# The last layer of a graph transformer: row normalisation, routing and ranking rearranged over the engines

## The reference

```python
def _layernorm(x, axis=-1, eps=1e-05):
    m = jnp.mean(x, axis=axis, keepdims=True)
    v = jnp.var(x, axis=axis, keepdims=True)
    return (x - m) / jnp.sqrt(v + eps)

probs = jax.nn.softmax(xf @ switch_w + switch_b, axis=-1)     # xf: 1250 normalised rows
prob_max = jnp.max(probs, axis=-1)
routes = jnp.argmax(probs, axis=-1)
sort_idx = jnp.lexsort((-prob_max, routes))
...
rank = jnp.zeros((N,), jnp.int32).at[sort_idx].set(rank_sorted.astype(jnp.int32))
keep = rank < capacity                                        # capacity 195 of 1250 rows
...
h = jax.nn.gelu(jnp.einsum('ecd,edf->ecf', buf[:E], w1) + b1[:, None, :], approximate=False)
o = jnp.einsum('ecf,efd->ecd', h, w2) + b2[:, None, :]
y = jnp.where(keep[:, None], y_exp, xf)
out = y * prob_max[:, None]
```

## Time and profile before

| | us |
|---|---|
| median of 3 runs | 1721.52 (1719.59 to 1725.29) |
| the profiled execution, its own time | 1720.55 |
| its span in the profile | 1718.8 |
| mark of tile 0 to start of `ranked` (L1703) | 1454.43 to 1559.10 |
| behind it, up to the end of the span | 159.7 |

### The profile page before, as it was taken

How to read it: one execution, slowest core, us unless ns; L and a number is a source line. 1 busy time by engine, 2 the same in 40 slices (tenths; PEclk the granted TensorE clock), 3 DMA queues, 4 the chain that set the end, 5 groups by cost and what they waited for, 6 DMA issues and landing times.

```text
span 1718.8 us, 25251 instructions
## 1 busy us (share of the span) xinstructions
PE 1582.5 (92%) x9809; PEld 1196.0 (70%) x9809; DVE 1135.0 (66%) x2618; ACT 680.6 (40%) x1359; POOL 412.0 (24%) x251
## 2 busy tenths in 40 slices
PE   3979999999989889999999999998999999986987
PEld 2556666555655568887888888888888976666664
DVE  6777664114466989898988697668765833785223
ACT  4421001122232466667767664336534521441110
POOL 3788888888400000000000000000000000002331
PEclk9999999999999999999999999999999999996999
DMA  9335535454752422223420264336312224645951
GB/s 360 83 60 118 119 77 118 61 92 74 198 178 85 143 76 84 88 80 102 134 81 28 64 191 144 125 108 202 131 47 79 88 83 146 220 180 201 315 160 50
DMA packets 194889, 213.67 MB, mean 124 GB/s; under 512 B 81359, under 2 KB 149597, under 8 KB 194770
## 3 DMA queue, kind: packets, MB, share of 16 engines
q1 hardware_dynamic: 118146, 187.01, 33.0%
q0 software_dynamic: 75760, 22.70, 8.3%
q10 hardware_dynamic: 864, 2.36, 0.4%
HBM read 144.74 MB, written 68.40 MB: 124 GB/s over the span
## 4 chain that ended last, share of the span: by engine, by line
PE 53%; POOL 16%; DVE 13%; DMA 7%; issue 6%; ACT 4%; SPq 0%; POOLq 0%; ACTq 0%; DVEq 0%
PE bank L1073 20%; POOL table L2117 16%; PE bank L902 6%; PE bank L904 6%; PE bank L903 6%; DMA table<-amount,place 4%; PE bank L1243 4%; PE bank L1231 3%; PE bank L1127 3%; PE bank L1099 2%; DVE junk L1478 2%; PE bank L1142 1%; DVE eb L1513 1%; PE bank L1112 1%; DVE eb L1522 1%
## 5 line engine op out<-in xcount | busy, mean ns | idle before, releaser
L1073 PE MATMUL bank<-hb,eb 128*128 128x193 f32 (+3 forms) x2400 | 417.7, 331 | 12.7 <-ACT node L1920 7.6
L1073 PEld LDWEIGHTS bank<-hb,eb 128*128 128x128 f32 (+3 forms) x2400 | 400.3, 190 | 23.3 <-issue 10.3
L2117 POOL DMA_INDIRECT table<-amount,place x170 | 346.9, 2040 | 73.3 <-issue 49.1
L2123 POOL IOTA iota8i<- 128x8 int32 x1 | 0.1, 140 | 952.7 <-DMA node_rows<-node 952.7
L1513 DVE SCALAR_TENSOR_TENSOR eb<-shift_b,as_low,shift_b 128x640 f32<-128x640 f32 (+1 forms) x240 | 196.5, 861 | 0.3 <-PE bank L1073 0.2
L1906 ACT ACTIVATE eb<-eb,asd 128x640 f32<-128x640 f32 (+1 forms) x240 | 181.4, 812 | 28.7 <-DVE eb L1513 28.7
L1478 DVE CUSTOM_DVE_ANT_0 junk<-ab,absent 128x1250 bf16<-128x1250 f32 x120 | 174.2, 1452 | 1.1
L1522 DVE SCALAR_TENSOR_TENSOR eb<-eb,count 128x1280 f32<-128x1280 f32 (+1 forms) x120 | 174.6, 1455 | 0.0
L902 PE MATMUL bank<-wg_hi,x1T_hi 128*128 128x384 bf16 (+3 forms) x360 | 118.6, 329 | 0.3 <-DVE x1T_lo L1345 0.3
L903 PE MATMUL bank<-wg_lo,x1T_hi 128*128 128x384 bf16 (+3 forms) x360 | 118.6, 329 | 0.0
L904 PE MATMUL bank<-wg_hi,x1T_lo 128*128 128x384 bf16 (+3 forms) x360 | 118.6, 329 | 0.0
(11 more groups left out here) (290 smaller groups left out, 3011.2 us busy)
## 6 DMA issues: line engine op xcount, KB each, us to landing
w<-in_w SPq DMA_DIRECT2D x16, 1152.0 KB, 10.1
shift_b<-shift_rows SPq DMA_DIRECT2D x24, 625.0 KB, 5.7
h_rows<-h_row SPq DMA_DIRECT2D x27, 388.0 KB
hb<-h_rows SPq DMA_DIRECT2D x12, 873.0 KB
ar<-node_rows SPq DMA_DIRECT2D x27, 384.0 KB
table<-zero POOLq DMA_DIRECT2D x3, 3054.0 KB, 19.0
tab<-table SPq DMA_DIRECT2D x27, 312.5 KB, 3.7
qk_rows<-qk_row SPq DMA_DIRECT2D x12, 625.0 KB
```

The costliest lines, as they stand in the source:

```text
L1073: ins = T.matmul(bank[w // 2][0:M, c0:c0 + GC + 1], p[0:K, u, w * P:w * P + M], hv[0:K, t, 0:GC + 1], start=opens and u == 0 and w % 2 == ...
L2117: G.indirect_dma_start(tables[i], bass.IndirectOffsetOnAxis(place[:, c:c + 1], axis=0), amount16[:, c:c + 1], None, compute_op=ALU.add).th ...
```

## The change

Four things change, all in the last layer.

1. The reciprocal root. Before, six small VectorE operations on one column (L1633 to L1643) made it, and VectorE then made the normalised row (L1645). Now there are five small ones, three of which take other columns as per-partition scalars, and the last makes the bias -mean/root. ScalarE makes the normalised row, as Identity with scale and bias from those columns.
2. The bias of the switch is added by TensorE, as a seventh matmul of each tile's logits with a row of ones. VectorE's addition and the step `logits` on VectorE go; `route` reads the logits from `bank`.
3. `rank` makes one comparison over all rows so far (larger or equal) in place of two (larger or equal for earlier tiles, larger for its own), and subtracts from the own tile's count the ties that are not earlier, by a mask with values 0 and -1.
4. Waits and counts are renumbered to match.

```diff
                 for k in range(KD):
-                    ins = T.matmul(bank[2][0:R, 0:EXPERTS], fT[t % 2][:, k, 0:R], sw[:, k, :], start=k == 0,
-                                   stop=k == KD - 1)
-                ins.then_inc(sem["logit_mm"], 1)
+                    T.matmul(bank[2][0:R, 0:EXPERTS], fT[t % 2][:, k, 0:R], sw[:, k, :], start=k == 0, stop=False)
+                T.matmul(bank[2][0:R, 0:EXPERTS], ones[0:1, 0:R], sbias[0:1, :], start=False,
+                         stop=True).then_inc(sem["logit_mm"], 1)
...
-                V.tensor_scalar(v, v, LN_EPS, None, ALU.add).then_inc(sem["x2_norm"], 1)
+                V.tensor_scalar(v, v, LN_EPS, -1.0, ALU.add, ALU.mult).then_inc(sem["x2_norm"], 1)
                 ve.wait_ge("x2_root", t + 1)
                 V.reciprocal(r, u).then_inc(sem["x2_norm"], 1)
                 ve.wait_ge("x2_norm", n + 2)
-                V.tensor_tensor(u, v, r, ALU.mult).then_inc(sem["x2_norm"], 1)
+                V.tensor_scalar(u, v, r, r, ALU.mult, ALU.mult).then_inc(sem["x2_norm"], 1)
                 ve.wait_ge("x2_norm", n + 3)
-                V.tensor_tensor(u, u, r, ALU.mult).then_inc(sem["x2_norm"], 1)
+                V.tensor_scalar(r, u, 3.0 / ROOT, r, ALU.add, ALU.mult).then_inc(sem["x2_norm"], 1)
                 ve.wait_ge("x2_norm", n + 4)
-                V.tensor_scalar(u, u, -0.5, 1.5, ALU.mult, ALU.add).then_inc(sem["x2_norm"], 1)
-                ve.wait_ge("x2_norm", n + 5)
-                V.tensor_tensor(r, r, u, ALU.mult).then_inc(sem["x2_norm"], 1)
-                ve.wait_ge("x2_norm", n + 6)
-                V.tensor_scalar(xf[0:R, t, :], x2[0:R, t, :], stats3[0:R, t, 12:13], stats3[0:R, t, 14:15],
-                                ALU.subtract, ALU.mult).then_inc(sem["xf_ready"], 1)
+                V.tensor_scalar(v, mean, -1.0, r, ALU.mult, ALU.mult).then_inc(sem["x2_norm"], 1)
...
             def route(t):
...
+                V.tensor_reduce(most, out, AX.X, ALU.max).then_inc(sem["route_v"], 1)
                 ve.wait_ge("iota_f", 3)
-                V.tensor_tensor(lg[0:R, t, :], bank[2][0:R, 0:EXPERTS], sbias[0:R, :],
-                                ALU.add).then_inc(sem["route_v"], 1)
...
-                for p0, p1, op, j in ((0, lo, ALU.is_ge, 0), (lo, hi, ALU.is_gt, 1)):
-                    if p1 > p0:
-                        ins = V.scalar_tensor_tensor(won[0:R, p0:p1], pr[0:R, p0:p1], prob, mate[0:R, p0:p1], op,
-                                                     ALU.mult, accum_out=cnt[0:R, j, t:t + 1])
-                ins.then_inc(sem["ranks"], 1)
+                V.scalar_tensor_tensor(won[0:R, 0:hi], pr[0:R, 0:hi], prob, mate[0:R, 0:hi], ALU.is_ge, ALU.mult,
+                                       accum_out=cnt[0:R, 0, t:t + 1]).then_inc(sem["ranks"], 1)
...
             def new_norm(t):                                  # ScalarE
-                se.wait_ge("x2_norm", 6 * t + 1)
-                A.activation(stats3[:, t, 15:16], stats3[:, t, 13:14], ACT.Sqrt).then_inc(sem["x2_root"], 1)
+                R = rows(t)
+                se.wait_ge("x2_norm", NORM_STEPS * t + 1)
+                A.activation(stats3[:, t, 15:16], stats3[:, t, 13:14], ACT.Sqrt, scale=-ROOT).then_inc(sem["x2_root"], 1)
+                se.wait_ge("x2_norm", NORM_STEPS * (t + 1))
+                A.activation(xf[0:R, t, :], x2[0:R, t, :], ACT.Identity, bias=stats3[0:R, t, 13:14],
+                             scale=stats3[0:R, t, 14:15]).then_inc(sem["xf_ready"], 1)
```

More of the change, by code:

```diff
@@ L60 @@
 WEIGHT_SETS = 5
-ROUTE_STEPS, RANK_STEPS = 7, 4
+ROUTE_STEPS, NORM_STEPS, RANK_STEPS = 6, 5, 4
+ROOT = 2.0 ** (2 / 3)
 OUT_ROWS = 4
@@ L616, in program @@
         lg, ex = put("lg", [P, NT, EXPERTS]), put("ex", [P, NT, EXPERTS])
-        earlier = put("earlier", [P, P])
+        uncount = put("uncount", [P, P])
         stats3 = put("stats3", [P, NT, 16])
@@ L727, in program @@
         even, win = put("even", [P, P], BF16), put("win", [P, P], BF16)
-        cnt = put("cnt", [P, 3, NT])
+        cnt = put("cnt", [P, 2, NT])
         signs = put("signs", [P, 2], BF16)
@@ L1629, in new_norm @@
                 R = rows(t)
-                v, r, u = (stats3[:, t, i:i + 1] for i in (13, 14, 15))
-                n = 6 * t
+                mean, v, r, u = (stats3[:, t, i:i + 1] for i in (12, 13, 14, 15))
+                n = NORM_STEPS * t
                 ve.wait_ge("x2", 3 * (t + 1))
-                V.tensor_scalar(v, v, LN_EPS, None, ALU.add).then_inc(sem["x2_norm"], 1)
+                V.tensor_scalar(v, v, LN_EPS, -1.0, ALU.add, ALU.mult).then_inc(sem["x2_norm"], 1)
                 ve.wait_ge("x2_root", t + 1)
@@ L1658, in route @@
                 n = ROUTE_STEPS * t
-                lt, et = lg[0:R, t, :], ex[0:R, t, :]
+                lt, et, out = lg[0:R, t, :], ex[0:R, t, :], bank[2][0:R, 0:EXPERTS]
                 most, prob, which, total = (pm[0:R, i, t:t + 1] for i in (0, 1, 2, 7))
+                ve.wait_ge("logit_mm", t + 1)
+                V.tensor_reduce(most, out, AX.X, ALU.max).then_inc(sem["route_v"], 1)
+                ve.wait_ge("iota_f", 3)
                 ve.wait_ge("route_v", n + 1)
[L1662 to L1667, removed]
+                V.tensor_scalar(et, out, most, None, ALU.subtract).then_inc(sem["route_v"], 1)
+                V.scalar_tensor_tensor(lt, out, most, iota8[0:R, :], ALU.is_lt, ALU.max).then_inc(sem["route_v"], 1)
+                ve.wait_ge("route_v", n + 3)
                 V.tensor_reduce(which, lt, AX.X, ALU.min).then_inc(sem["route_v"], 1)
@@ L1670, in route @@
                 V.tensor_reduce(total, et, AX.X, ALU.add).then_inc(sem["route_v"], 1)
-                ve.wait_ge("route_v", n + 6)
+                ve.wait_ge("route_v", n + 5)
                 V.reciprocal(prob, total).then_inc(sem["route_v"], 1)
@@ L1697, in rank @@
                 ve.wait_ge("ranks", n + 3)
-                V.scalar_tensor_tensor(win[0:R, 0:R], even[0:R, 0:R], 1.0, earlier[0:R, 0:R], ALU.mult, ALU.mult,
-                                       accum_out=cnt[0:R, 2, t:t + 1]).then_inc(sem["ranks"], 1)
+                V.scalar_tensor_tensor(win[0:R, 0:R], even[0:R, 0:R], 1.0, uncount[0:R, 0:R], ALU.mult, ALU.mult,
+                                       accum_out=cnt[0:R, 1, t:t + 1]).then_inc(sem["ranks"], 1)
             def ranked(_):
@@ L1791, in vector_program @@
                         x_bias=x_bias, row_split=row_split, row_add=row_add,
-                        expert_setup=expert_setup, new_x=new_x, new_norm=new_norm, logits=logits, route=route,
+                        expert_setup=expert_setup, new_x=new_x, new_norm=new_norm, route=route,
                         rank=rank, ranked=ranked, mapped=mapped, own=own_, slots_turn=slots_turn,
@@ L2020, in route @@
                 R = rows(t)
-                se.wait_ge("route_v", ROUTE_STEPS * t + 3)
+                se.wait_ge("route_v", ROUTE_STEPS * t + 2)
                 A.activation(ex[0:R, t, :], ex[0:R, t, :], ACT.Exp).then_inc(sem["route_exp"], 1)
@@ L2126, in expert_setup @@
                 G.iota(iota_i[:, :], pattern=[[1, WIDEST]], base=0, channel_multiplier=0).then_inc(sem["iotas"], 1)
-                G.memset(earlier[:, :], 1.0).then_inc(sem["pool_set"], 1)
+                G.memset(uncount[:, :], 0.0).then_inc(sem["pool_set"], 1)
                 ge.wait_ge("pool_set", 9)
-                G.affine_select(out=earlier[:, :], in_=earlier[:, :], compare_op=ALU.is_gt, fill=0.0, base=0,
+                G.affine_select(out=uncount[:, :], in_=uncount[:, :], compare_op=ALU.is_gt, fill=-1.0, base=0,
                                 pattern=[[-1, P]], channel_multiplier=1).then_inc(sem["pool_set"], 1)
```

## The result

The changed kernel took 1731.01 us (median of 6 runs, 1728.57 to 1732.12), the one before 1721.96 (6 runs, 1719.59 to 1725.41). The ratio is 1.005, with an interval of 1.0037 to 1.0064: slower by 0.5%, or 6.4 to 11 us. The profiled execution took 1728.57 us against 1720.55, 8.0 more.

A forecast was written before the change was run, and what follows sets the result against it. No single engine was taken as the bound, but a per-tile loop through VectorE's probability and TensorE's matmuls. Terms of +0.40, +3.19, -3.20, +4.2 and +0.7 made +5.3 us on 1721.52: 1726.8, range 1722.3 to 1730.6.

The forecast's parts named there:

- own case: Whole kernel: the forecast's main case, +5.3 us to 1726.8, between 1724 and 1728.5; chance 0.70.
- the rival of the staying stall: Mark 4 to 5: most of the 3.2 us isn't regained, or other gaps drop the clock; 1730.0; chance 0.18.
- five terms: Mark 1 +0.40, marks 1 to 4 +3.19, mark 4 to 5 -3.20, marks 5 to 9 +4.2, tail +0.7 us.
- The loop step: Each tile, mark to L1672: the Exp's table load comes out behind ScalarE's Identity, +1.16 us.
- A pause behind the load: ScalarE, rival: the Exp waits another 1.28 us after each table load, 1738.3 us in all; chance 0.03.
- Marks 1 to 4: Three intervals: 3 x 1.16 less a wait of 0.29 for `mi`, +3.19 us.
- The stall is swallowed: Mark 4 to 5: TensorE's wait for tile 6's features shrinks and the clock stays up; 10.84 for 14.04, -3.20 us.
- Marks 5 to 9: Four intervals: 4 x 1.16 less 0.4 for comparisons and VectorE's lateness, +4.2 us.
- Tail: Mark 9 to the rank of tile 8: +1.16 less two comparisons (0.25) and the last bias (0.2), +0.7 us.
- Bias and comparison: TensorE's bias +0.23 hidden, VectorE's 0.20 saved only in the last tile; one comparison saves 0.13 where VectorE is late.
- The step that was mis-sized: Up to mark 1: no route yet, TensorE's turn of `xf` waits and `xf` comes later, +0.40 us.

The follow-up runs named there:

- late-weights pair: Kernel before and changed kernel, each with the weights of experts 1 and 2 issued behind the tile loop; ratios 0.9993 and 1.0043 against the kernel before.
- the spare matmuls: Changed kernel plus twelve matmuls with unused results on TensorE, ahead of its wait for tile 0's normalised row; ratio 1.0031 against the kernel before.

## Why the prediction was right, and where it was small

- *The number.* 0.5% by the ratio is 1730.1 us on the forecast's base of 1721.52: inside the stated 1722.3 to 1730.6, but above the own case's 1724 to 1728.5. The raw median, 1731.01, lies 0.4 above the range; before's median beside it was 0.4 higher than the forecast's base. The range reached up to there for the rival of the staying stall (1730.0), and the stall did not stay. So the mechanism and four of the five terms were right, but that the time lies inside the range is in part luck: the loss was forecast at 5.3 us and measured at 8.6 by the ratio.
- *The loop step.* Predicted +1.16 from mark to L1672, by Identity (1.01), a load started 0.02 behind it, an Exp right behind the load. Measured 4.21 against 3.08, +1.13. The Identity starts 1.43 after the mark (laid out: 1.47). The cause is shown from both sides: load moved ahead, 3.15; Exp moved ahead, 2.20; row back on VectorE, 2.67. VectorE's idle time in front of L1659 was 1.95 (predicted: about 1.8).
- *A pause behind the load.* The Trainium skill, "ScalarE: Activation LUTs", "What ACT_TABLE_LOAD costs", adds 1.38 us for a drain; the trace has 0.01 (the load ends at 1479.19 + 1.28 = 1480.47, the Exp starts at 1480.48). The measurement decides: no such pause stands on this path.
- *Marks 1 to 4.* +3.19 predicted, +3.13 measured (32.17 against 29.04).
- *The stall is swallowed.* -3.20 predicted, -3.24 measured (10.80 against 14.04), and no wait for `ar` there (predicted: 0.5). The late-weights pair confirms it was slack: moving the weights takes 4.4 from that interval of before and nothing from the changed kernel's.
- *Marks 5 to 9.* +4.2 predicted, +4.18 measured (43.82 against 39.64). *Tail.* +0.7 predicted, +0.64 measured.
- *Bias and comparison* cost nothing, as said. Their gain in the loop of before, had they come alone, would have been eaten by waits for `ar`; the prediction didn't speak of that.
- *The step that was mis-sized* is the first: "TensorE's turn of `xf` was what waited (1.56): +0.40". It was +2.06. The turn did come 0.38 later (gap 1.94 in place of 1.56), but in this profile the clock then fell for about half a tile, and 1.66 more were lost. Five profiles have this gap, and in three of them the clock fell; where it stayed up, the interval was 9.30, or +0.39, as predicted. So the term lacked a fall of the clock with a chance, not a certain cost. The rival of the staying stall named "other gaps, now longer by up to 1.1 us a tile, let the clock fall"; it was priced as the other side of the stall, not as a term beside a stall that goes. With the spare matmuls in the gap the interval was 1.74 shorter.
- *The rest.* 5.3 predicted. In the profiled pair: 2.06 + 3.13 - 3.24 + 4.18 + 0.64 = 6.77 inside the stretch, 0.61 by a later mark 0, 0.32 from `ranked` to the span's end and 0.32 outside the span, together 8.02. Nothing in the change is known to touch the 0.61 and the 0.32 behind `ranked`, and both numbers move by more between profiles of other kernels here. The 0.32 outside the span do belong to the change. In every execution of every kernel with the new root, TensorE's bias and the single comparison together, the time is 2.04 to 2.22 us longer than the span. In the kernel before, with early or late weights, and in those with only the row or only bias and comparison changed, it is 1.69 to 1.87. The prediction had no term for that, and its cause stays open.
- *From the profiled pair to the medians.* Within each kernel the executions with the lower mean granted clock took longer. Of the changed kernel, 1728.57 us went with 0.976, 1730.16 with 0.974, and 1732.00 and 1731.87 with 0.971. The profiled one has the highest clock and the shortest time of the six, so the rows above show less loss of clock than its median execution had. Where in the other executions the clock fell, and how much of that the change causes, no trace here shows.

## What to carry to other kernels

A table load belongs to the instruction in front of which it stands: work put between two functions of different sets pushes the load behind itself, and a load that was hidden comes out on the path (here 1.13 us a tile for a load of 1.28). Before moving work to an engine that is idle on average, lay out that engine's own order around the move and ask what waits behind it. And a loop that gets faster meets the next wait: here the row on VectorE with the other parts of the change gave nothing in total with the weights in the loop and 5.9 us with the weights behind it, and one stall had hidden 3.2 us of a loss.

## What the runs showed that was not expected

Whether a wait on TensorE cost its own length or some 1.7 us more could not be read off its length. In the thirteen profiles TensorE waited 17 times for `ar` by 0.76 us or more (up to 3.02), each time right behind the logits' matmuls (8 columns). Behind 13 of these waits the granted clock fell to its lower level, with a mean of 0.77 to 0.89 over the interval: behind one of 0.76, the interval took 11.59 us, against 9.58 in the kernel before. Behind the other four, of 0.90, 0.94, 1.32 and 2.06, it stayed up. Gaps behind matmuls of 384 columns were no surer guide: 1.35 and 1.56 us left the clock up in all seven profiles that have them, 1.94 or 1.95 in two of five. And twice (the row alone, mark 7 to 8; the changed kernel with late weights, mark 8 to 9) the clock fell with no wait for `ar`, behind waits that left it up in the changed kernel. What decides it stays open. For a forecast this means a term with a chance for each gap of about a microsecond or more, and for an experiment that one profile of a kernel isn't enough to say what a stop costs.
